# Attention in a macaron block: the masks of two head groups written to PSUM by VectorE and ScalarE instead of by TensorE

## What is computed

```python
qkv = jnp.einsum('bsi,oi->bso', x, w_qkv)          # x: layer-normed, 16 heads of 8
scores = jnp.einsum('bhqd,bhkd->bhqk', q, k) / jnp.sqrt(jnp.asarray(HD, x.dtype))
allowed = (j <= i) & (i - j < WINDOW)              # WINDOW = 64
scores = jnp.where(allowed[None, None], scores, jnp.asarray(-jnp.inf, x.dtype))
attn = jax.nn.softmax(scores, axis=-1)
ctx = jnp.einsum('bhqk,bhkd->bhqd', attn, v)
out = jnp.einsum('bso,po->bsp', ctx, w_out) + b_out
```

## Time and profile before

| What | us |
|---|---|
| Median of 3 runs | 583.62 |
| Lowest and highest of them | 582.66, 587.52 |
| The profiled execution, its own time | 588.97 |
| Its span, first to last instruction | 587.2 |
| TensorE busy, share of the span | 498.9, 85% |
| VectorE busy | 443.3, 75% |
| GpSimd busy | 310.6, 53% |
| ScalarE busy | 271.2, 46% |

### The profile page before, as it was taken

How to read it: one execution, slowest core, us unless ns; L and a number is a source line. 1 busy time by engine, 2 the same in 40 slices (tenths; PEclk the granted TensorE clock), 3 DMA queues, 4 the chain that set the end, 5 groups by cost and what they waited for, 6 DMA issues and landing times.

```text
span 587.2 us, 10082 instructions
## 1 busy us (share of the span) xinstructions
PE 498.9 (85%) x3866; PEld 301.8 (51%) x3866; DVE 443.3 (75%) x882; ACT 271.2 (46%) x419; POOL 310.6 (53%) x232
## 2 busy tenths in 40 slices
PE   3997899999999899998887798887778868788995
PEld 2775677676767768766432233332223323235674
DVE  4479678667678545676692978999989989999652
ACT  1433655656556423664587536334333333330732
POOL 3158121201200002377300977999999999995573
PEclk9998998898898679999796688999979879899988
DMA  7000000000000000000009543353744335200011
GB/s 206 2 0 2 3 2 2 2 3 3 2 2 3 1 1 2 2 0 2 0 5 348 237 161 131 140 197 155 292 187 170 144 143 196 89 2 0 2 36 37
DMA packets 12323, 42.74 MB, mean 73 GB/s; under 512 B 2858, under 2 KB 8755, under 8 KB 10227
## 3 DMA queue, kind: packets, MB, share of 16 engines
q1 hardware_dynamic: 11458, 41.56, 18.4%
q10 hardware_dynamic: 816, 0.53, 0.3%
HBM read 40.78 MB, written 1.31 MB: 72 GB/s over the span
## 4 chain that ended last, share of the span: by engine, by line
PE 46%; POOL 16%; issue 15%; DVE 14%; ACT 7%; DMA 1%; POOLq 0%; ACTq 0%; DVEq 0%
POOL hC L994 9%; PE bk L444 6%; PE bk L455 6%; PE bk L660 5%; DVE hst L923 5%; PE bk L646 5%; PE bk L1077 4%; PE bk L635 3%; PE bk L834 3%; PE bk L623 2%; DVE xnT L278 2%; POOL dBu L977 2%; ACT g L759 2%; POOL powers L292 1%; PE bk L440 1%
## 5 line engine op out<-in xcount | busy, mean ns | idle before, releaser
L1077 PE MATMUL bk<-hC,ident 128*128 128x512 f32 x256 | 134.7, 660 | 21.5 <-POOL hC L994 16.1
L994 POOL TENSOR_TENSOR hC<-hst,rows 128x1024 f32<-128x1024 f32 x63 | 146.5, 2351 | 9.6 <-DVE hst L923 9.6
L923 DVE TENSOR_TENSOR_SCAN hst<-bk,dBu 128x1024 f32<-128x1024 f32 x64 | 144.2, 2274 | 2.2 <-POOL dBu L977 2.2
L1166 ACT ACTIVATE bk<-delta,aneg 128x1024 f32<-128x1024 f32 x64 | 71.5, 1118 | 112.7 <-DVE hst L923 112.1
L285 POOL TENSOR_TENSOR veps<-mv,lneps 128x4 f32<-128x4 f32 x24 | 5.2, 218 | 173.4 <-DVE mv L257 173.3
L1077 PEld LDWEIGHTS bk<-hC,ident 128*128 128x128 f32 x256 | 50.9, 209 | 85.3 <-issue 49.0
L495 ACT ACTIVATE rows<-bk 128x512 f32<-128x512 f32 x64 | 38.2, 597 | 72.2 <-PE bk L444 72.2
L906 DVE TENSOR_TENSOR dBu<-bk,du 128x1024 f32<-128x1024 f32 x48 | 57.8, 1204 | 12.7 <-PE bk L1057 12.1
L533 DVE TENSOR_REDUCE smax<-bk 128x4 f32<-128x512 f32 x64 | 43.7, 682 | 28.0 <-PE bk L635 28.0
L759 ACT COPY g<-bk 128x512 f32<-128x512 f32 x64 | 37.4, 585 | 52.6 <-PE bk L646 51.9
L646 PE MATMUL bk<-ident,g 128*128 128x128 f32 x256 | 45.5, 309 | 2.6 <-ACT g L753 2.6
(11 more groups left out here) (161 smaller groups left out, 769.4 us busy)
## 6 DMA issues: line engine op xcount, KB each, us to landing
rows<-c_rows SPq DMA_DIRECT2D x16, 2048.0 KB, 7.2
rows<-c_rows SPq DMA_DIRECT2D x4, 1024.0 KB, 9.6
x<-in_x_dram SPq DMA_DIRECT2D x4, 256.0 KB, 5.2
out_dram<-x SPq DMA_DIRECT2D x4, 256.0 KB, 2.3
wmoe<-in_w_dram ACTq DMA_DIRECT2D x2, 256.0 KB, 5.9
wup<-in_upT_dram SPq DMA_DIRECT2D x1, 256.0 KB
wdn<-in_downT_dram SPq DMA_DIRECT2D x1, 256.0 KB
wproj<-in_in_wT_dram SPq DMA_DIRECT2D x1, 256.0 KB
```

The source lines that it names most:

```text
L923: nc.vector.tensor_tensor_scan(hst[k % 3][:, :], dA[k % 2][:, :], dBu[k % 3][:, :], 0.0, ALU.mult, ALU.add).then_inc(m2["scan"], 1)
L994: nc.gpsimd.tensor_tensor(hC[k % 4][:, :], hst[k % 3][:, :], crep[:, k % 12, :], ALU.mult).then_inc(m2["hC"], 1)
L1077: last = nc.tensor.matmul(bk01[:, r * CH:(r + 1) * CH], ident[:, :], hC[k % 4][:, r * CH:(r + 1) * CH], start=(k % NS == 0), stop=(k % NS ...
L1166: nc.scalar.activation(dA[k % 2][:, :], delta[:, i, :], ACT.Exp, scale=aneg[:, h * NS + n:h * NS + n + 1]).then_inc(m2["dA"], 1)
```

## The change

For every tile but the first, the masks of groups 0 and 1 are no longer written by TensorE. `mask_scores` returns at once for them. VectorE writes the mask of group 0 into `bank[0]` (`write_masks`, a copy with a cast from bf16 to f32, semaphore `mkd`), between `context(t - 1)` and `soften(t, 2)`. ScalarE writes that of group 1 into `bank[1]` (`write_mask`, semaphore `mka`), between `copy_ctx(t - 1)` and `probs(t, 2)`. `scores(t + 1)` waits for both semaphores in addition. The score matmuls are as before and add to what stands in the bank. The masks of groups 2 and 3, and all four of the first tile, stay with TensorE. No loads, buffers or bank assignments change.

```diff
--- before.py
+++ after.py
@@ -212,7 +212,7 @@
         ter1 = Ffn("ter1", True, wup, wdn, ACT.Gelu)
 
         at = {k: sem("at_" + k) for k in (
-            "full", "free", "qm", "bias", "s", "max", "sub", "p", "pt", "pts", "pv", "rden", "cx", "cxt", "cxs", "op", "xupd")} | layer_norm_semaphores("at")
+            "full", "free", "mkd", "mka", "qm", "bias", "s", "max", "sub", "p", "pt", "pts", "pv", "rden", "cx", "cxt", "cxs", "op", "xupd")} | layer_norm_semaphores("at")
         m1 = {k: sem("m1_" + k) for k in (
             "xT", "proj", "xb", "tap", "cstep", "conv", "u", "g")} | layer_norm_semaphores("m1")
         m2 = {k: sem("m2_" + k) for k in (
@@ -525,7 +525,18 @@
                                                qmask[:, a:a + 1].to_broadcast([P, CH]), ALU.mult)
             last.then_inc(at["qm"], 1)
 
+        BY_VECTOR, BY_SCALAR = (0,), (1,)
+
+        def masks_of(t):
+            first = int(t % TPB == 0)
+            return mask1[:, first:first + 1, :].to_broadcast([P, HPG, P])
+
         def attn_vector(dve):
+            def write_masks(t):
+                for j in BY_VECTOR:
+                    nc.vector.tensor_copy(bank[j][:, :].rearrange("p (a k) -> p a k", a=HPG), masks_of(t)
+                                          ).then_inc(at["mkd"], 1)
+
             def soften(t, j):
                 s3d = bank[j][:, :].rearrange("p (a k) -> p a k", a=HPG)
                 if j == 0:
@@ -559,6 +570,8 @@
                 soften(t, 1)
                 if t > 0:
                     context(t - 1)
+                if t + 1 < NT:
+                    write_masks(t + 1)
                 soften(t, 2)
                 soften(t, 3)
                 if t > 0:
@@ -617,6 +630,8 @@
                 last.then_inc(at["full"], 1)
 
             def mask_scores(t, j):
+                if t > 0 and j in BY_VECTOR + BY_SCALAR:
+                    return
                 if t > 0:
                     pe.wait_ge(at["sub"], t * JG - JG + j + 1)
                 first = int(t % TPB == 0)
@@ -627,6 +642,10 @@
             def scores(t):
                 c, b, r = t // TPC, t // TPB, t % TPB
                 pe.wait_ge(at["free"], 5 * c + 3)
+                if t > 0 and BY_VECTOR:
+                    pe.wait_ge(at["mkd"], t * len(BY_VECTOR))
+                if t > 0 and BY_SCALAR:
+                    pe.wait_ge(at["mka"], t * len(BY_SCALAR))
                 if c > 0:
                     pe.wait_ge(at["qm"], c)
                 for a in range(HPG):
@@ -758,6 +777,11 @@
                     act.wait_ge(at["pv"], t * JG - JG + j + 1)
                 nc.scalar.copy(pT[:, j, :], psPT[j % 2]).then_inc(at["pts"], 1)
 
+            def write_mask(t, j):
+                act.wait_ge(at["sub"], t * JG - JG + j + 1)
+                nc.scalar.copy(bank[j][:, :].rearrange("p (a k) -> p a k", a=HPG), masks_of(t)
+                               ).then_inc(at["mka"], 1)
+
             def copy_ctx(t):
                 act.wait_ge(at["cxt"], t + 1)
                 if t > 0:
@@ -784,8 +808,12 @@
                     take_v(c + 1, 1)
                 if t > 0:
                     copy_ctx(t - 1)
+                if t + 1 < NT and 1 in BY_SCALAR:
+                    write_mask(t + 1, 1)
                 probs(t, 2)
                 probs_t(t, 1)
+                if t + 1 < NT and 2 in BY_SCALAR:
+                    write_mask(t + 1, 2)
                 probs(t, 3)
                 probs_t(t, 2)
                 if ahead and i == 1:
```

## The result

| | before | changed |
|---|---|---|
| Median of 4 runs each | 583.14 | 596.0 |
| Lowest and highest | 581.81, 587.52 | 591.55, 600.7 |
| Profiled execution, span | 588.97, 587.2 | 594.55, 592.8 |
| Its mean granted clock over the span | 0.916 | 0.912 |

The ratio of the runs is 1.0179, 95% interval 1.0116 to 1.0241, so the change makes the kernel slower, by 1.2% at least; the interval has 2% inside it. Run again beside other versions, the changed kernel had a median of 596.0 once more (6 runs), against 584.37 (29 runs); ratio 1.0143, interval 1.0077 to 1.0210.

What follows compares the result with a forecast made beforehand. TensorE was taken to set the pace over most of a tile, but group 2's exponential to decide at the changed place. 2.7 + 1.8 + 0.6 + 0.5 + 0.8 = 6.4 us longer gave 590.0 us, range 583.0 to 596.0.

Steps and rivals of the forecast that it cites:

- What bounds: Attention, between projection and transposes of group 2: the wait ending last decides, and it differs between two kinds of tile.
- Removed: 30 mask matmuls off TensorE, 15 pairs of 0.44 us: 6.6 us if TensorE were the bound there.
- Sizes of the writes: Mask writes before group 2's exponential and maximum: ScalarE's taken as 0.48 us, VectorE's as 0.61 us.
- Nine tiles with a piece: Tiles with a piece of the next chunk: ScalarE's write delays group 2's exponential, +0.30 us each, 2.7 us in sum.
- Tiles 8, 12, 14: Tiles without a piece: VectorE's write delays the subtraction of group 2, +0.61 us each, 1.8 us in sum.
- Tile 0: First tile, without `copy_ctx`: ScalarE's write delays the exponential the transposes wait for, by 0.48 us.
- Tiles 4 and 13: Tiles without a piece, at half clock at this place: VectorE's write costs +0.30 us each, 0.6 us in sum.
- Two more waits: TensorE's two added semaphore waits before the scores: 0.05 us by estimate, 0.8 us over 15 tiles.
- rival 1: TensorE's clock gets worse, with dense matmuls removed and idling added: four more half-clock stretches, 594.8 us; chance 0.20.
- Rivals 2 and 3: Better clock, all five half-clock stretches vanishing: 584.0 us, chance 0.20; TensorE the bound after all: 580.4 us, chance 0.08.
- The TensorE-bound rival: Group 2's exponential not late in the nine tiles, saving 0.44 us each: 580.4 us; chance 0.08.

Runs made afterwards that it cites:

- Experiments 1 and 2: The changed kernel with only VectorE's mask write (1) or only ScalarE's (2), TensorE writing the other masks: medians 587.35 and 586.59 us.
- Experiment 4: The changed kernel without the two engines' writes: from tile 1 on nobody writes the masks of groups 0 and 1; median 577.2 us.
- experiment 3: The changed kernel with TensorE writing the masks of groups 0 and 1 again, behind the other engines' writes; median 589.25 us.
- 7: The changed kernel with both writes moved: ScalarE's ahead of the copy of transposed group 0, VectorE's behind the subtraction of group 3; median 584.32 us.
- 6: The unedited kernel of experiment 3 run again beside the changed kernel; median 588.63 us.

## Why the prediction was right, and where it was short

The direction and the cost of the longer tiles were right, and for the reason given. The total was not close: 596.0 lies at the very end of the stated range of 583.0 to 596.0, 6 us above the forecast and above the 592.2 that its own bounds allowed. The missing term is the clock.

*What bounds.* Right: the place between the projection and the transposes of group 2 decides, and which wait ends last there differs between two kinds of tile. Experiments 1 and 2 separate the two chains, ScalarE's in nine tiles and VectorE's in five.

*Removed.* Right that the 6.6 us were not to be had. Experiment 4 shows 0.17 us per tile with a piece and nothing in the quiet ones.

*Sizes of the writes.* From the write to the next instruction ScalarE's takes 0.52 us (132.12 to 132.64; I had 0.48) and VectorE's 0.59 (139.05 to 139.64; I had 0.61). The row nearest in shape was a good guide for both, and neither a faster copy on VectorE nor a quicker write to PSUM on ScalarE, which the prediction weighed, showed.

*Nine tiles with a piece.* 0.30 forecast, 0.34 measured (9.06 against 8.72), the 0.04 being the size of the write. *Tiles 8, 12, 14.* 0.61 forecast, 0.59 measured. *Tile 0.* 0.48 forecast; experiment 3's tile 0 ran at full clock in 8.73 us against 8.21, +0.52. *Tiles 4 and 13.* Priced at half clock in the profile at hand, 0.30. At full clock tile 13 costs 0.59 as its likes do; a price taken at a place where the clock happened to be low does not hold for an execution in which it is high.

*Two more waits.* 0.8 us forecast, none measured: from the mask pair to the scores it is 0.53 us in tile 7 (133.83 to 134.36), as before.

The tiles add up to 9 x 0.34 + 5 x 0.59 + 0.52 = 6.5 us at full clock; the sum was 6.4. That the two are so close is partly luck: the 0.8 us for waits that did not come nearly made up for 0.4 too little in the nine tiles and 0.6 in tiles 4 and 13.

*The clock, rival 1.* This is the term that was mis-sized. I gave the forecast no clock at all and the worse clock a chance of 0.20 at 594.8; it is what came. With 109 to 115 us of half-clock time against 95, at 0.3 us each, the changed kernel loses 4 to 6 us to it, and 6.5 + 4 to 6 is 10.5 to 12.5, where the medians say 12.9 and 11.6. Rival 1 had the size about right as well: four more stretches of 3.4 us, 14 us at half clock, for 4.8 us. Its reason, matmuls taken out and idling added, fits the runs, with one thing to add: missing matmuls without the late writes (experiments 4 and 7) and the late writes with the matmuls kept (3 and 6) leave the mean clock where it was or a little higher, 0.920 to 0.926. Whether it takes both or only enough idling stays open. The Trainium skill ("TensorE: Matmul & The Clock Gate", on the gate) says that the full clock is kept by sustained activity. The runs agree in part: with the same delays the clock is 0.926 where matmuls fill the idle time and 0.903 to 0.908 where nothing does, but in experiment 4, with less TensorE work than before, it is 0.925.

*Rivals 2 and 3.* The better clock did not come with the change; the best means, 0.926, came with the delays and the kept matmuls. The TensorE-bound rival is excluded by the 13.2 us of idling before the transposes and by experiment 4, where even without the writes the pair brings 0.17 us and not 0.44.

## What to carry to other kernels

Work taken off the busiest engine is worth only what that engine would not have waited for anyway: look at what ends last behind it. When it is given to other engines, the place in their queues matters more than its length; 0.5 us on ScalarE ahead of the exponential that is waited for delayed it by 0.5 us, and three instructions earlier, in idle time, by nothing. And a matmul in TensorE's idle time may hold the clock up: before removing it, price the half-clock time, from many runs, not one.

## What was not expected

The versions with the same delays, one with 30 short matmuls more, differ by 7 us in the median: 596.0 against 588.6 and 589.3. The one that does more work on TensorE is the faster. The changed kernel's runs also spread wider, 589.21 to 605.87 in one set of 6, where the kernel before had 579.58 to 589.13 in 29.
